# x by features on GpSimd from the third batch on, a new order on VectorE and fill between the sums of q

## The reference

```
normed = gamma * x / |x| * sqrt(128)
q, k, v = normed @ w_q / 4, normed @ w_kv          # 8 heads of 16
phi(u) = [1, u, u_i * u_j / sqrt(2)]
state = sum_n phi(k)_n (x) v_n ;  den = phi(q) . sum_n phi(k)_n
x = layernorm(x + (phi(q) @ state / max(den, eps)) @ w_out)
h = silu(x @ w1 * s1) * (x @ w2 * s2)              # 512 wide
h = gelu(h @ h1 * hs1) ; h = gelu(h @ h2 * hs2)
out = layernorm(x + h @ w3 * s3)
```

## Time and profile before

| | |
|---|---|
| median of 3 runs | 564.23 us (562.71 to 565.49) |
| profiled execution | 565.74 us |
| its span, first to last instruction | 563.9 us |
| PE, DVE, ACT, POOL busy | 545.4, 457.1, 460.5, 159.5 us |
| mean granted clock of PE | 0.987 |

### The profile page before, as it was taken

One profiled execution on the slowest core, in us unless ns is written; L12 is line 12 of the kernel. 1 busy time (PEld: TensorE's weight loads), 2 busy tenths in 40 slices (PEclk: granted clock), 3 DMA queues, 4 the chain that ended last, 5 costly groups with the idle time before them and its releaser, 6 DMA issues.

```text
span 563.9 us, 11483 instructions
## 1 busy us (share of the span) xinstructions
PE 545.4 (97%) x3608; PEld 410.3 (73%) x3608; DVE 457.1 (81%) x982; ACT 460.5 (82%) x954; POOL 159.5 (28%) x246
## 2 busy tenths in 40 slices
PE   7879999999999999999999999999999999999994
PEld 3446877878687787868778786877878787786772
DVE  5776769888787988878798887879888787968764
ACT  4757797988979798897979889797988979787773
POOL 3541414223151422314142222414222241400000
PEclk9799999999999999999999999999999999999998
DMA  8000000000000000000000000000100000000000
GB/s 274 18 22 2 19 2 2 20 19 20 20 19 19 0 19 19 19 19 19 19 0 19 18 19 19 19 19 0 29 8 19 19 19 19 1 19 1 20 1 37
DMA packets 7366, 12.25 MB, mean 22 GB/s; under 512 B 816, under 2 KB 1840, under 8 KB 7344
## 3 DMA queue, kind: packets, MB, share of 16 engines
q1 hardware_dynamic: 7056, 11.86, 6.6%
q10 hardware_dynamic: 288, 0.10, 0.1%
HBM read 7.77 MB, written 4.19 MB: 21 GB/s over the span
## 4 chain that ended last, share of the span: by engine, by line
PE 89%; issue 4%; ACT 2%; DVE 2%; POOL 1%; DMA 1%; SPq 0%; POOLq 0%; DVEq 0%
PE fps L431 28%; PE fps L434 27%; PE ring L368 7%; PE ring L398 5%; PE ring L348 5%; PE ring L322 4%; PE ring L407 3%; PE ring L415 2%; PE ring L329 2%; PE fps L476 1%; PE fps L423 1%; PE ring L309 1%; PE ring L355 1%; DMA w_raw<-in_w 1%; PE ring L378 1%
## 5 line engine op out<-in xcount | busy, mean ns | idle before, releaser
L431 PE MATMUL fps<-hid_hi,w_hi 128*128 128x512 f32 x576 | 229.7, 399 | 0.0
L434 PE MATMUL fps<-hid_lo,w_hi 128*128 128x512 f32 x576 | 226.9, 394 | 1.3 <-DVE hid_lo L944 0.9
L709 ACT ACTIVATE hid_hi<-fps,col 128x512 fp32r<-128x512 f32 x128 | 90.3, 705 | 54.1 <-PE fps L434 54.1
L431 PEld LDWEIGHTS fps<-hid_hi,w_hi 128*128 128x128 f32 x576 | 108.3, 188 | 25.4 <-issue 3.4
L434 PEld LDWEIGHTS fps<-hid_lo,w_hi 128*128 128x128 f32 x576 | 108.3, 188 | 25.0 <-DVE hid_lo L944 2.2
L944 DVE TENSOR_TENSOR hid_lo<-fps,hid_hi 128x512 fp32r<-128x512 f32 x128 | 88.2, 690 | 32.4 <-ACT fps L711 30.8
L711 ACT ACTIVATE fps<-fps,col 128x512 f32<-128x512 f32 x128 | 86.6, 677 | 0.0
L660 ACT ACTIVATE phiT<-ring 128x512 f32<-128x512 f32 x127 | 77.2, 636 | 5.1 <-PE ring L348 4.0
L930 DVE SCALAR_TENSOR_TENSOR h<-fps,col,gate_zo 128x512 f32<-128x512 f32 x64 | 47.8, 748 | 38.7 <-ACT gate_zo L696 34.5
L257 DVE TENSOR_TENSOR phi_k<-phi_k 128x896 f32<-128x896 f32 x64 | 69.1, 1085 | 0.2 <-ACT v_one L633 0.2
L348 PE MATMUL ring<-qT,sel 128*128 128x512 f32 x128 | 52.9, 417 | 3.5 <-ACT v_one L633 2.0
(11 more groups left out here) (100 smaller groups left out, 902.3 us busy)
## 6 DMA issues: line engine op xcount, KB each, us to landing
x_b<-in_x SPq DMA_DIRECT2D x16, 256.0 KB, 2.6
out<-gate_zo SPq DMA_DIRECT2D x16, 256.0 KB, 2.0
w_raw<-in_h SPq DMA_DIRECT2D x2, 1024.0 KB, 9.4
w_raw<-in_w SPq DMA_DIRECT2D x3, 256.0 KB, 4.6
sel_raw<-in_sel SPq DMA_DIRECT2D x1, 320.0 KB, 6.0
w_qkv_raw<-in_w_kv SPq DMA_DIRECT2D x1, 128.0 KB, 2.8
const<-in_consts ACTq DMA_DIRECT2D x1, 92.0 KB, 3.0
w_qkv_raw<-in_w_q SPq DMA_DIRECT2D x1, 64.0 KB, 2.8
```

What stands on the lines that cost most here:

```text
L431: nc.tensor.matmul(fps[:, bank, :], w[:, o:o + P], hi, start=start, stop=False)
L434: return nc.tensor.matmul(fps[:, bank, :], w[:, o:o + P], lo, start=False, stop=stop)
L709: nc.scalar.activation(hid[1 - layer][0][:, m, :], fps[:, bank, :], ACT.Gelu, scale=scale)\
```

## The change

- From batch 2 on PE no longer transposes x. The host passes x a second time, by features (xT). SP loads it into x_cols. POOL's norms rn of the batch go to a buffer in DRAM and come back as one row, the same on all partitions (rn_row); POOL then makes xnT_hi = x_cols * rn_row (rounded), x_scaled = the same product in full, and xnT_lo = x_scaled - xnT_hi (`normed_cols`). PE's first projection waits for that. ACT's x_hi and DVE's x_lo stay in steps 0 and 1 only.
- The token order becomes the natural one: x for the norms (x_nrm) and x for the residual (x_res) are loaded apart, and out is stored in rows of 128 features where four rows were in one run.
- POOL: normed_cols stands behind spread_rest and ahead of k_small(t, 0); the norm of t+1 ahead of k_small(t, 1).
- DVE: x_lo leaves; sum_squares moves ahead of the first GELU tile; q_lo(0) stands behind tile 1, the sum of x1 and q_lo(1) behind tile 2, the variance of x1 and phi_k 0 and 1 behind tile 3.
- ACT: square(t+1) moves ahead of the first GELU; in step 0 the first reading of low bits moves behind the sums of q.
- PE: in step 0 one dummy of 512 columns behind project_q and dummies of 128 columns behind sums 2 to 6. In step 1 five sums and the two rests of q of batch 1 take the place of four dummies of 512 columns, with short dummies behind three sums; step 2 keeps sums 5, 6 and 7 and gets a dummy of 256 columns.

```diff
@@ module: writes_before counts "xT" for two batches @@
+FIRST_ONLY = {"xT": 2}
@@ SP @@
+            def load_norm_parts(n):
+                sp.wait_ge(sq_ready, n)
+                sp.dma_start(x_nrm[:, :, :], x_d[bass.ds(n, 1)].rearrange("b p j d -> (b p) j d"))\
+                    .then_inc(nrm_loaded, 16)
+            def load_cols(n):
+                if is_positive(n - 2):
+                    sp.wait_ge(x_scaled_ready, n - 2)
+                sp.dma_start(x_cols[:, :], xT[bass.ds(n, 1)].rearrange("b d n -> (b d) n")).then_inc(cols_loaded, 16)
+            def spread_norms(n):
+                sp.wait_ge(rn_ready, n + 1)
+                sp.dma_start(rn_d, rn[:, :]).then_inc(rn_stored, 16)
+                sp.wait_ge(rn_stored, 16 * (n - 1))
+                sp.dma_start(rn_row[:, :], rn_all).then_inc(rn_row_loaded, 16)
+            def load_residual(n):
+                if is_positive(n):
+                    sp.wait_ge(ring_free[bank_of(RING, "out")], read(RING, n, "out"))
+                sp.dma_start(x_res[:, :, :], x_res_d[bass.ds(n, 1)].rearrange("b p j d -> (b p) j d"))\
+                    .then_inc(res_loaded, 16)
             def step(t, par, front, middle, ffn, tail):
                 if front and not is_step(t, B - 1):
-                    if middle:
-                        sp.wait_ge(ring_free[bank_of(RING, "out")], read(RING, t, "out"))
-                    sp.dma_start(x_b[1 - par][:, :, :],
-                                 x_d[bass.ds(t + 1, 1)].rearrange("b p j d -> (b p) j d")
-                                 ).then_inc(x_loaded[1 - par], 16)
+                    if not is_step(t, 1):
+                        load_norm_parts(t + 1)
+                    load_cols(t + 1)
+                    if not is_step(t, 1):
+                        spread_norms(t + 1)
+                if front:
+                    load_residual(t)
+                if is_step(t, 1):
+                    spread_norms(2)
@@ PE @@
             def project_kv(t, j):
-                if j == 0:
+                if j == 0 and not is_step(t, 0) and not is_step(t, 1):
+                    pe.wait_ge(x_lo_ready, t - 1)
+                elif j == 0:
                     pe.wait_ge(ring_free[bank_of(RING, "xT")], read(RING, t, "xT"))
...
+                if is_step(t, 0) and 2 <= f < 7 or is_step(t, 1) and 2 <= f < 5:
+                    keep_busy(P)
...
                     if is_step(t, 2):
-                        sums_of_q(1, 0)
-                        sums_of_q(1, 1)
-                        rest_of_q(1, 0)
-                        sums_of_q(1, 2)
                         transpose_x1(1, 0)
+                        sums_of_q(1, 5)
+                        keep_busy(256, 3)
...
-                    if front:
-                        transpose_x(t)
+                    if is_step(t, 0):
+                        transpose_x(0)
@@ PE, second_step @@
                 project_out(1)
-                for _ in range(4):
-                    keep_busy(N)
+                sums_of_q(1, 0)
+                sums_of_q(1, 1)
+                rest_of_q(1, 0)
+                for f in (2, 3, 4):
+                    sums_of_q(1, f)
+                rest_of_q(1, 1)
@@ DVE, step @@
-                if front:
-                    x_lo(t)
...
+                if front and not is_step(t, B - 1):
+                    sum_squares(t + 1)
                 if ffn:
                     gelu_tile(t, 0, 0)
-                if front:
-                    phi_k_main(t, 0)
-                if ffn:
                     gelu_tile(t, 0, 1)
                 if front:
-                    q_lo(t, 0, 1)
+                    q_lo(t, 0)
                 if ffn:
                     gelu_tile(t, 0, 2)
                 if middle:
-                    sum_x1(t, 1 - par)
+                    sum_x1(t)
+                if front:
+                    q_lo(t, 1)
                 if ffn:
                     gelu_tile(t, 0, 3)
-                if front:
+                if middle:
+                    var_of_x1(t)
+                if front:
+                    phi_k_main(t, 0)
                     phi_k_main(t, 1)
                 if ffn:
                     gelu_tile(t, 1, 0)
@@ DVE, second_step @@
-                phi_k_main(1, 0)
-                sum_x1(1, 0)
-                q_lo(1, 0)
-                norm_scale(0, x1p, mv, rstd, mv_ready, rstd_ready, x1[0], x1_ready)
-                q_lo(1, 1)
+                q_lo(1, 0, 1)
+                sum_x1(1)
+                var_of_x1(1)
+                sum_squares(2)
+                norm_scale(0, x1p, mv, rstd, mv_ready, rstd_ready, x1[0], x1_ready)
+                phi_k_main(1, 0)
                 x1_lo(1)
@@ POOL @@
+            def normed_cols(t):
+                pool.wait_ge(cols_loaded, 16 * (t - 1))
+                pool.wait_ge(rn_row_loaded, 16 * (t - 1))
+                pool.wait_ge(ring_full, written(RING, t - 1, "qT"))
+                nc.gpsimd.tensor_tensor(xnT_hi[:, :], x_cols[:, :], rn_row[:, :], ALU.mult).then_inc(x_hi_ready, 1)
+                nc.gpsimd.tensor_tensor(x_scaled[:, :], x_cols[:, :], rn_row[:, :], ALU.mult).then_inc(x_scaled_ready, 1)
+                pool.wait_ge(x_scaled_ready, t - 1)
+                pool.wait_ge(x_hi_ready, t + 1)
+                nc.gpsimd.tensor_tensor(xnT_lo[:, :], x_scaled[:, :], xnT_hi[:, :].bitcast(F32), ALU.subtract)\
+                    .then_inc(x_lo_ready, 1)
...
                 if front:
+                    normed_cols(t)
                     k_small(t, 0)
                 if tail:
                     inv_std(t - 3, zveps_ready, zveps, zrstd, zrstd_ready)
+                if front and not is_step(t, B - 1):
+                    norm_of_x(t + 1)
                 if front:
                     k_small(t, 1)
                 if middle:
                     inv_std(t - 1, veps_ready, veps, rstd, rstd_ready)
-                if front and not is_step(t, B - 1):
-                    normed_x(t + 1, 1 - par)
```

More of the change, by code:

```diff
@@ L767, in step @@
                     copy_kv(t, 3)
+                if ffn and front and not is_step(t, B - 1):
+                    square(t + 1)
                 if ffn:
@@ L776, in step @@
                 if is_step(t, 1):
-                    load_table(ACT.Silu)
+                    square(2)
                 if front:
@@ L797, in step @@
                     x1_hi(t)
-                if front and not is_step(t, 1):
+                if front:
                     square_sums(t, 4)
@@ L1140, in _ @@
             pool.wait_ge(consts_loaded, 16)
-            normed_x(0, 0)
-            peeled(step, 0)
+            normed_x(0, x_nrm[:, :, :])
+            k_small(0, 0)
+            k_small(0, 1)
+            normed_x(1, o_b)
             spread_rest(1)
```

124 lines of the change are left out of this document (72 added, 52 removed).

## The result

| | before | after |
|---|---|---|
| median of 5 runs | 564.23 us (562.71 to 565.92) | 560.36 us (559.62 to 561.24) |
| profiled execution | 565.74 us | 561.24 us |
| its span | 563.9 us | 559.4 us |
| ratio to before | 1 | 0.9927, 95% interval 0.9901 to 0.9953 |

A forecast was written before the change was run, and what follows sets the result against it. PE's queue was taken to bound steps 3 to 15. Terms -6.2 + 0.65 (x1) - 1.5 - 3.5 + 0.2 (norm row) + 0.2 (store) = -10.1 us gave 554.1 us, range 551.5 to 560.5.

The forecast's parts named there:

- 1: PE, steps 2 to 15: four transposes of x leave, 0.44 us a step, 6.2 us in all.
- 2: POOL makes x's halves: three operations of 1.15 us, chain 3.7, ready 2.3 to 2.6 us early; PE pays nothing.
- Rival C: POOL becomes the bound: chain over 6.3 us, PE waits at each first projection; 595 us at 2.3 each; chance 0.07.
- 3: DMAs behind x, including the norm row: price 0, from 0 to +0.5 us once, at step 2; sum carries +0.2.
- 4: DVE's new order: PE waits 0.05 us a step for x1 (0 to 0.15), 0.65 us over 13 steps.
- Rival B: x1 waits every step, POOL's root sitting out both DVE phi_k products: 0.5 us each, 560 us; chance 0.12.
- 5: First steps: step 0 gains 1.5 us if PE's clock holds; steps 1 and 2 gain 3.5 us.
- Rival A: First steps: clock or branch leaves 1 to 2 us of 5, dummies not holding clock; 557 to 558; chance 0.15.
- 6: The end: output stored in runs of 512 B, last store costs +0.2 us (0 to 1).

The follow-up runs named there:

- pool_two: Changed kernel with two extra full-width products on POOL ahead of its three operations in every step from 2 on: 571.91 us, ratio 1.0142.
- no_branch: Changed kernel without PE's read of the low-bits sum and its branch, going straight into the rounded program: 561.52 us, ratio 0.9955.
- cover: Changed kernel with the old order of PE, ACT and Silu table in steps 1 and 2, four dummies ahead of the branch: 561.89 us, ratio 0.9955.
- norm_early: Changed kernel with POOL making the norms of batch 2 before its wait for x1: 560.32 us, ratio 0.9936.
- gap_fill: Changed kernel with five more dummy products of 512 columns ahead of PE's branch: 558.51 us, ratio 0.9905.
- read_early: Changed kernel with the low-bits wait and read ahead of the sums of q of batch 1, branch left in place: 560.52 us, ratio 0.9934.
- before_fill: Kernel before with only the dummy products of step 0 added: 563.02 us, ratio 0.9980.

## Why the prediction was right or wrong

**1, right.** The steady step is 32.38 us (state applied at 84.80 and at 473.36, 12 steps) where it was 32.78: 0.40 a step, which is the 0.44 of the transposes less 0.04.

**2, right, with one duration low.** The operations take 1.30, not 1.15; the fixed part and the width that I had weighed (1.25) were the better estimate than the row of the one-input multiply. No steady step waits for POOL. The Trainium skill, page "GPSIMD Engine Reference", section "Engine selection", has GpSimd at about half of VectorE's speed for such work. The trace agrees (1.30 against 0.69 us for a 128x512 operation with two inputs), and yet the move paid, for PE was the bound. pool_two marks where PE begins to wait: 2.67 us further. Rival C's threshold of 6.3 us for the chain was 0.6 low: from POOL's start at 243.09 to PE's at 250.01 it is 6.9.

**3, wrong in the step on the norm row of step 2, and this is what no_branch and cover pay.** The changed kernel itself doesn't: POOL is done at 54.89 and PE comes at 55.72. The prediction had the row at 46.5 to 48, so rn at 42 to 42.5, and POOL ready at 50.1 to 51.7. With PE on the forecast's schedule (no_branch) they were 49.77 and 54.4. Three terms were short: rn itself, queued on POOL behind k_small, which DVE's products stretched (43.94); the load, 3.7 us in place of 2 to 3 (the store took 2.1); the three operations, 4.6 in place of 3.7. Each was given alone, and the price of 0.2 left no room for their sum, 3.5 us against the middle of the forecast. In the steady steps the row takes 4.4 us to land by the page, more than forecast too, but there it has the time.

**4, right in time.** Forecast 0.05 us a step; 0.04 is missing, and PE's weight loads show it (waits of the changed kernel: engine, line, total, times, longest):

```profile
PEld fps L479 <- DVE x L943: 2.8, 13, 0.3
```

The idle time on the loads is 0.26 us in one step and 0.16 in the next, in turn, and set side by side the two kinds of step show what PE loses: the product behind the transposes of x1 starts 21.87 us after the application at 214.33, and 21.77 after that at 246.73, where it was 21.78 before. So one step in two takes 32.40 to 32.44 us and the other 32.32 to 32.35: 0.1 us every second step makes the 0.04. The weight loads of those two steps:

```profile
235.79 0.42 PEld L479 LDWEIGHTS fps<-const,x 128*128 128x128 f32 x4 [0.26 <-DVE x L943]
```

```profile
268.04 0.47 PEld L479 LDWEIGHTS fps<-const,x 128*128 128x128 f32 x4 [0.17 <-DVE x L943]
```

Rival B's mechanism is there: the reciprocal root takes 1.78 to 1.81 us in 14 of 16 steps where it took 1.01. POOL and DVE of the changed kernel:

```profile
264.42 1.81 POOL L1200 TENSOR_TENSOR rstd<-veps,const 128x4 f32<-128x4 f32 x1 [3.92 <-DVE veps L965]
```

```profile
264.27 2.09 DVE L277 TENSOR_TENSOR phi_k<-phi_k 128x896 f32<-128x896 f32 x2
266.29 0.68 DVE L1009 TENSOR_TENSOR hid_lo<-fps,hid_hi 128x512 fp32r<-128x512 f32 x1
266.89 1.10 DVE L943 TENSOR_SCALAR x<-x1p,mv,rstd 128x128 f32<-128x128 f32 x4
```

It ends at 266.23 and is wanted at 266.89. It sits out the rest of the first phi_k product and none of the second; that is the argument which had given B 0.12. The Trainium skill, page "SBUF — State Buffer", section "SBUF: two separate sides", has the loser wait to the end of the other's instruction. The trace agrees by the durations: 0.80 us lost where 0.9 of the first product were left.

**5, wrong, and this is the miss.** The step that failed is the pricing of the first steps, -1.5 and -3.5 us: it took PE's branch as covered and the clock as held, and x1 as ready where it was. The runs showed +0.51 us to the first application and +0.14 from there to the second, 6.05 us short together.

Step 0 was to bring 1.5 us. With the clock held all the way (norm_early, whose step 0 is that of the changed kernel) the state is applied at 24.89, 0.87 earlier than before. The strided copies of batch 0, which I had not priced, start everything 0.3 late, where x_hi(0) was to bring 0.3: ACT comes to the copy of the state at 22.95 in place of 22.6 to 22.7. (The terms as the prediction writes them add up to 23.0; 22.6 follows when ACT's instructions are counted by their starts, and ACT does take 2.38 us there, from 20.57 to 22.95.) Another 0.2 lies between that copy and the application (1.94 us, 1.74 before). In the profiled execution of after the first projection stands 0.4 later than in norm_early (10.87 against 10.47), and the clock was low from about 12.5 to 15.9 us, behind the longer wait for xnT_lo, which cost some 1.0 us more and made it +0.51.

Steps 1 and 2 were to bring 3.9. The prediction did name the branch and put it at 2 us (3.5 to 1.5), but as a bound, not as the likeliest case, although the edit removes exactly the four dummies that stood ahead of the branch. Branch and clock each cost 1.5 us (no_branch, gap_fill against after), together 3.0; without either the stretch is 2.9 us shorter than before where 3.9 was forecast. Of the 1.0 left, 0.75 is x1: in no_branch it is ready 13.04 us after the first application, before it was 12.29, since DVE now makes both halves of q_lo ahead of the sum of x1 (0.33) and its scale starts 0.54 us behind the end of POOL's root in place of 0.11, for which no run gives the cause. The rest goes with the three phi_k products, 3.75 us in no_branch beside POOL's k_small where they took 3.08 before; the last part of the state waits 0.34 for them.

Rival A, the clock or the branch, had the right mechanism for some 4.0 of the 6.05 us (branch 1.5, clock 1.5 and 1.0), with a loss well over its 3 to 4. Its reason, that the dummies do not hold the clock, is not borne out: the falls came ahead of them and in the branch's gap.

**6, right in its range (0 to 1), 0.2 too much.** The stretch from the last application to the end is as long as before; the last store itself costs 0.27 us more.

The changed kernel's time of 560.4 is also what rival B gave, for another reason: a time that agrees with a case does not show the case. What was forecast for the change, 1.8%, was reached by none of the kernels run: with the branch covered, the norms early and batch 0 in natural order the kernel takes 556.84 us, 0.9878 of before (0.9851 to 0.9906), the best of them.

## What to carry to other kernels

Before you put a stretch of useful work in the place of filler, ask what the filler hid: here it hid a jump of 2 us, and without it the clock was low for 6.8 us in place of 3.5. Where two chains end within a microsecond of each other, price the second one with all its queues at the new schedule of the first, and add up its short terms with their errors, not one by one. And shifting work on one engine can lengthen what runs beside it on another, so a slack read from the trace is good only for the place where it was read. A start-up in which the clock falls in some executions and not in others can't be judged by one trace of each kernel.

## What the runs showed of the hardware

- PE's branch into its copy of the program for the later steps costs 2.06 us beyond the wait for data, 1.19 with the value read early (read_early); 4.45 us of dummies ahead of it leave no gap in PE's work.
- PE's clock fell from 2.4 to 1.2 GHz behind idle stretches of PE: it was low from 12.5 to 15.9 behind 1.5 us (10.87, after), from 39.8 to 46.6 in the branch's gap of 4 us (after), from 54.7 to 58.1 behind 2.7 us (54.44, no_branch). In the branch's gap, 3.1 to 4.2 us long, it fell in all eight kernels whose profile has it; behind the 1.5 us at the first projection in four of eleven. Held in step 0 (before_fill), it still fell behind the wait of step 2.
- The kernel before takes between 562.2 us at a mean granted clock of 0.997 and 566.1 at 0.983; in between the mean clock doesn't order its executions fully (563.06 at 0.988, 563.04 at 0.993). What decides in which execution the clock falls stays open.
- A copy from PSUM of 128x512 that writes every fourth element takes 1.08 us on ACT and 1.07 on DVE, where the dense one takes 0.6 and 0.7.
- A tiny operation on POOL (128x4, 1.01 us) takes 1.78 to 1.85 us beside a phi_k product of DVE; for rstd 1.81 is the median of 16.
